# Scatters of rows to the experts: three ahead of the additions of even units, two ahead of those of odd ones

## The reference, cut to what matters

```
xn = layernorm(x)
x  = x + segment_sum(edge_weight * (xn @ W)[dst], src) + b + linear_attention(xn)
y  = layernorm(x)
logits = y @ Wg + bg + bias;  two best of 8 experts per row, softmax of the two as weights
x  = x + sum over the two experts of weight * (relu(y @ W1[e] + b1[e]) @ W2[e] + b2[e])
```

## Time and profile before

| What | us |
|---|---|
| median of three runs | 3717.16 |
| the profiled execution | 3712.03 |
| its span, first to last instruction | 3710.3 |
| PE (TensorE matmul) busy | 2723.5 (73%) |
| DVE (VectorE) busy | 2553.0 (69%) |
| POOL (GpSimd) busy | 2548.0 (69%) |
| ACT (ScalarE) busy | 628.5 (17%) |
| additions to `out` (L823), 210, GpSimd's time for one | 1.580 |
| scatters to `x_sorted` (L805), 196, GpSimd's time for one | 0.978 |

### The profile page before, as it was taken

How to read it: one execution, slowest core, us unless ns; L and a number is a source line. 1 busy time by engine, 2 the same in 40 slices (tenths; PEclk the granted TensorE clock), 3 DMA queues, 4 the chain that set the end, 5 groups by cost and what they waited for, 6 DMA issues and landing times. The chain is left out here.

```text
span 3710.3 us, 69265 instructions
## 1 busy us (share of the span) xinstructions
PE 2723.5 (73%) x16161; PEld 2235.5 (60%) x16165; DVE 2553.0 (69%) x6668; ACT 628.5 (17%) x1326; POOL 2548.0 (69%) x2390
## 2 busy tenths in 40 slices
PE   1447776577777777676676667667767999999998
PEld 1346666366566665555555555555533788888887
DVE  9999999455555555677777777777768566654444
ACT  8312222411111111000000000000013221112221
POOL 7347777677777777777777777777745477775444
PEclk9987777789999999888899898998877999999999
DMA  5545555634444444444444444444457455555443
GB/s 173 167 144 183 180 184 158 222 117 128 127 125 128 125 124 126 131 131 125 131 131 131 129 127 131 131 131 124 125 177 220 73 115 114 112 114 92 73 75 52
DMA packets 327621, 492.01 MB, mean 133 GB/s; under 512 B 60714, under 2 KB 247854, under 8 KB 327214
## 3 DMA queue, kind: packets, MB, share of 16 engines
q0 software_dynamic: 127584, 270.17, 28.9%
q1 hardware_dynamic: 161029, 176.37, 15.6%
q10 hardware_dynamic: 38601, 41.04, 3.5%
HBM read 376.35 MB, written 111.03 MB: 131 GB/s over the span
## 5 line engine op out<-in xcount | busy, mean ns | idle before, releaser
L770 POOL DMA_INDIRECT message<-h_table,records x1616 | 1549.9, 959 | 511.5 <-issue 498.4
L1278 PE MATMUL bank<-message,select 128*128 128x256 f32 x3232 | 924.5, 436 | 566.7 <-issue 296.6
L1278 PEld LDWEIGHTS bank<-message,select 128*128 128x128 f32 x3232 | 665.4, 215 | 781.7 <-issue 404.2
L1821 DVE TENSOR_SCALAR select<-iota_n,records 128x128 f32<-128x128 f32 x1660 | 594.3, 358 | 501.4 <-PE bank L1278 486.9
L1829 DVE TENSOR_TENSOR acc<-acc,bank 128x256 f32 x1660 | 683.4, 412 | 9.9 <-PE bank L1278 6.0
L823 POOL DMA_INDIRECT out<-acc,row_of x210 | 331.7, 1580 | 302.5 <-DVE acc L2356 152.5
L735 POOL DMA_INDIRECT lists<-placed,dest_i x300 | 348.5, 1162 | 201.2 <-ACT placed L957 106.9
L1514 PE MATMUL bank<-w,acc 128*128 x1680 | 387.1, 384 | 19.7 <-DVE acc L2340 19.7
L1501 PE MATMUL bank<-fx_t,acc 128*128 128x256 f32 x1680 | 380.1, 379 | 2.5 <-ACT fx_t L1096 2.5
L1514 PEld LDWEIGHTS bank<-w,acc 128*128 128x128 f32 x1680 | 315.6, 193 | 61.5 <-issue 21.5
L1501 PEld LDWEIGHTS bank<-fx_t,acc 128*128 128x128 f32 x1680 | 318.7, 190 | 46.0 <-ACT acc L1103 1.9
(11 more groups left out here) (356 smaller groups left out, 3579.2 us busy)
## 6 DMA issues: line engine op xcount, KB each, us to landing
fetched<-h_table SPq DMA_DIRECT2D x3200, 1.0 KB
fetched<-h_table ACTq DMA_DIRECT2D x2432, 1.0 KB
rows<-block_dram SPq DMA_DIRECT2D x75, 514.5 KB
acc<-x_sorted SPq DMA_DIRECT2D x105, 260.0 KB, 3.1
message<-h_table,records POOLq DMA_INDIRECT x1616
xt_in<-xt_dram SPq DMA_DIRECT2D x98, 256.0 KB
lists<-zeros_list SPq DMA_DIRECT2D x8, 1664.0 KB, 14.9
read_back<-lists SPq DMA_DIRECT2D x13, 1024.0 KB, 7.0
```

What stands on the lines that cost most here:

```text
L770: pool.indirect_dma_start(out=message[:, k % SETS, j, :], out_offset=None, in_=h_table, in_offset=Offset(ap=records[:, k * SET + j, 0:1], ...
L1278: last = nc.tensor.matmul(ps, select[:, slot % 2, j, :], rows_of, start=True, stop=True)
L1821: return V.tensor_scalar(select[:, k % 2, j, :], iota_n[:, :], records[:, k * SET + j, 1:2].bitcast(F32), records[:, k * SET + j, 2:3].bit ...
```

## The change

Odd units get two places for scatters and not three; the first scatters come one unit earlier, so SyncE's first table beside the units does too; the blanks come ten units later.

```diff
-    SEND_AT = [None, None, 3] + [ROUTE_FIRST + ROUTE_PACE * (t - 3) + 7 for t in range(3, TURNS)]
-    BLANKS_AT = SEND_AT[TURNS - 1] + 10
+    SEND_AT = [None, None, 2] + [ROUTE_FIRST + ROUTE_PACE * (t - 3) + 7 for t in range(3, TURNS)]
+    BLANKS_AT = UNIT_FROM[TURNS - 1] - 15
     TABLE_AT = [None, None] + [SEND_AT[t] + 8 for t in range(2, TURNS - 1)] + [SEND_AT[TURNS - 1] + 13]
-    assert PAIRS == TURNS * TURN and UNITS <= P and KH == 4 and BLANKS_AT + 12 < UNIT_FROM[TURNS - 1]
+    assert PAIRS == TURNS * TURN and UNITS <= P and KH == 4 and BLANKS_AT + 11 < UNIT_FROM[TURNS - 1]
...
             for u in range(UNITS):
                 if u >= SEND_AT[FIRST_PARTS]:
-                    for _ in range(3):
+                    for _ in range(3 - u % 2):
                         if waiting and u >= SEND_AT[waiting[0][0]]:
```

## The result

The changed kernel takes **3685.73 us** (median of five runs, 3684.89 to 3694.17) against 3711.85 for the kernel before (five runs, 3705.58 to 3720.75): ratio 0.9933, 95% interval 0.9915 to 0.9951. The profiled execution took 3685.73 us, its span is 3684.0, 26.3 less than before.

A forecast was written before the change was run, and what follows sets the result against it. TensorE bounds the kernel at 7.35 us a unit, with 28 us lost waiting behind GpSimd. Profiled 3712.0 - 28 + 3.5 = 3687.5; against the median, 3717.2 - 24.5 = 3692.7 us; range 3684 to 3707.

The forecast's parts named there:

- The sum: Whole kernel: profiled 3712.0 less 28 us of TensorE's losses plus 3.5 of remaining stall, 3687.5; against the median, 3692.7.
- The slack: From unit 78's second addition landing to unit 82's `down`: 12.4 us to spare, 5.3 us from landing to `down` already taken off.
- The step with the landing in it: GpSimd's two-scatter units: the next addition also waits for the unit's landing, so 6.8 us rather than 6.4.
- The last rival: Odd units on GpSimd: later landings eat the saving, each costing 0.6 us more, 17 us in all, to 3734; chance 0.04.
- the likeliest case: Tables beside the units: additions issued earlier escape the table write, keeping the lag at 5 to 7; 3692.7 us, chance 0.55.
- the first rival: Tables beside the units: all catch the additions, 12 us of stalls stay and 16 are won, 3701 us; chance 0.33.
- the step that failed: Second addition due 2 to 3 us after a table write begins: escaping costs about 1 us, being caught 5.
- The other steps are nothing: Earlier first scatters, blanks at 62 and SyncE's load of unit 10: hidden, cost 0; tables counted as before.

The follow-up runs named there:

- short tables: Table writes cut to the units of their turn (42 numbers for most, not 384): on the changed kernel ratio 0.9902, repeated 0.9901; on the kernel before 0.9913.
- third tables: Changed kernel with each table write cut to 42 partitions, 126 numbers in place of 384: 3676.66 us in one run.
- the tables at another moment: Changed kernel with SyncE beginning each table write only when a certain unit's additions have landed: ratio 0.9943, median 3689.55 us.

## Why the prediction was right, and where it wasn't

**The total.** Forecast 3692.7, measured 3685.7, inside the range of 3684 to 3707, but the nearness is partly luck. The sum had 24.5 us, all of it in the units; there the two traces have 18.7 and 18.2, and the medians have 26. The 7 us or so beside that had no term in the sum, and the traces don't place them. Ahead of unit 0 the start varied from 2885 to 2902 us over all kernels that write each table once, the same kernel's by 9 (the one before) and by 12 (the changed one with short tables). Whether the stages ahead run a little faster by chance, or the before kernel's other executions stall more than its two traces, is open.

The median gains of the short tables (32 and 39 us against 28.5 possible) are too large for the units as well, and for them the traces show a place. The edit shortens the two tables ahead of the units too. From the write of the first of these to `down` of unit 0 it took 69.8 to 71.8 us in the four traces with short or third tables, 74.6 to 81.0 in the nine with full ones, and 90.7 with each written twice.

**The bound.** Right: TensorE's 7.35 us a unit is the floor, 28 us above it were to be won, and the short tables reached it (603.0). The slack holds as well: with short tables at the old pace there was no stall up to a lag of 12.2, and at 14 to 15 `down` waited under 1 us each time. VectorE has no more routing steps there, and from a late landing to `down` it took 3.9 us at unit 51 of the kernel before (3288.07 + 10.23 to 3302.24) and not 5.3, which makes the slack 13.8.

**The pace.** A pair of units was to take 14.45 us. From unit 14 to unit 22 it took (3067.85 - 3008.97) / 4 = 14.72, TensorE's own 14.7; from unit 4 to 12 (2991.84 - 2934.04) / 4 = 14.45. So the new pace stops the growth, and takes back between nothing and 0.12 us a unit. The step with the landing in it (6.8, and not 6.4, for a two-scatter unit) was right: unit 15 took 6.98. The last rival, in which this wait eats all, is out.

**The signs.** By its own signs the likeliest case did not come: the wait of `down` for relu was to fall under 5 us and fell to 6.3, the units were to take 603 to 608 us and took 612.5. And the additions at the second to fourth table took 8 to 10.7 us, its sign that the first rival is right.

**The tables: the step that failed.** "At one end it escapes, the next unit's addition lands when the table is done anyway, and the table costs about 1 us" was taken as the likelier. It rested on a gap that the trace before does not have. "No addition was in flight that was due so early in a table write" looks at second additions only; first additions, issued at 3003.62 and 3165.37, 1.0 and 1.4 us ahead of their writes and so due some 2.5 to 3 us behind their starts, took 10.7 and 8.9 us to land.

```profile
DMA to landing us min/median/max: 10.7/10.7/10.7
DMA to landing us min/median/max: 8.9/8.9/8.9
```

Unit 12 did escape, at 3.7 of lag, as worked out. But the next additions were caught in its place and landed 8 to 9 us from their own issue, 1.4 us later than that step had it (+11.9 against +10.5 from the write's start), and the table cost 6.2 - 2.8 = 3.4 us. Without those 1.4 it would still have been 2.0 and not "about 1". At table three in this trace a second addition due 3.1 us after the write's start was caught at 10.7, and the lag went from 6.1 to 12.1. The five tables cost 4.3, 3.4, 6.0, 5.7 and 5.2 us of lag. So the first rival, all of them caught, describes the rest: it gave a lag of 10.9 and a stall of 5.7 plus 2.1 at table four, and the trace has 11.3 and 5.3 plus 2.5; and 12 us in all left over, where 9.8 were. It had the mechanism from table three on; the likeliest case had the nearer number, by the part that the units don't explain.

The Trainium skill's rule that stood for that rival ("DMA: Bandwidth & Descriptors", queues, rings and completion order: an increment lands only after the engine's earlier writes) agrees with what escaped and what didn't: unit 12's landing, 1.1 us behind the start, was through, the one due at 3.1 wasn't. It agrees too with that one's data, whose last packet ended 3.8 us ahead of its landing. It does not cover all that is seen, since with the tables at another moment the data itself was held, down to 2 GB/s.

**The shifts.** "The other steps are nothing" was wrong for one of them. I counted the first table one unit earlier as the same cost at another unit. It left 4.9 us of lag; at unit 11 it left 6.2 with all else equal, and table two then met unit 12: units 612.5 and 613.4 with the table at 10 and 619.5 with it at 11, ratios 0.9933 and 0.9971. The blanks at 62 are issued with nothing but the 0.30 us between issues ahead of them, as forecast. Without the earlier scatters and the later blanks the units took some 5 to 6 us more in one trace (618.7), which the ratios don't set apart from chance.

## What to carry to other kernels

A lag that grows by 0.3 us a unit is harmless until something takes the slack at one stroke: find the strokes first, since shortening them was worth 26 us at the old pace (631.4, the mean of two traces, to 605.6), and the whole change on top 2.6. A DMA of a few hundred single 4-byte numbers to DRAM beside a stream that others wait for should write only the numbers that will be read. And where a queue recovers slower than it is disturbed, a shift of one unit can decide a chain of stalls, so the worth of the parts of a change can't be added up (here 5.6 and -1.4 us of units alone, 18.7 together). And before a gap in a trace is filled by a guess, look at every instance of the event in it: the row that answered this one was there.

## What the runs showed of the hardware

- A write of 384 numbers of 4 bytes (1.5 KB) to DRAM from 128 partitions took 8.7 to 11.5 us until the read that waits for it; 126 numbers took 4.6 to 7.6 beside the units (8.1 once ahead of them), and 42 numbers 2.6 to 4.4.
- Beside the write of 384, second additions of another queue took 8.0 to 11.6 us to land where 4 is usual, and a first one up to 12.6. An addition issued 1.84 us or more ahead of the write escaped, one issued from 1.5 us ahead to 3.9 behind was caught.
- What is held depends on the moment. Issued 1.0 us ahead of the write, an addition had its data moved by +5.9 and landed at +9.7; issued 2.7 us behind it, its last packet ended at +11.7 and it landed at +12.1, while the core's DMA traffic was between 2 and 68 GB/s for 8 us (3083.75 to 3091.75).
- Later issue brought later landing, about half a us for each us.
